# Holding back SyncE's first loads until earlier ones have landed, in a conditional MLP kernel

## What is computed

```
out_nr = gelu(x @ w1_nr + b1_nr) @ w2_nr + b2_nr
out_tsr = gelu(x @ w1_tsr + b1_tsr) @ w2_tsr + b2_tsr
h = gelu(gelu(x @ w1_sr + b1_sr) @ w2_sr + b2_sr)
out_sr = h @ w3_sr + b3_sr
y = x + (out_nr, out_tsr or out_sr, by the batch's condition)
out = (y - mean(y)) * rsqrt(var(y) + 1e-5) * gamma + beta
```

## Time and profile before

| | us |
|---|---|
| median of 3 runs (lowest, highest) | 559.55 (559.47, 559.73) |
| the profiled execution, its own time | 559.85 |
| its span, first to last instruction | 558.1 |
| TensorE busy | 549.3 (98%) |
| VectorE, GpSimd, ScalarE busy | 273.9, 249.7, 213.4 |

### The profile page before, as it was taken

How to read it: one execution, slowest core, us unless ns; L and a number is a source line. 1 busy time by engine, 2 the same in 40 slices (tenths; PEclk the granted TensorE clock), 3 DMA queues, 4 the chain that set the end, 5 groups by cost and what they waited for, 6 DMA issues and landing times. The chain is left out here.

```text
span 558.1 us, 8218 instructions
## 1 busy us (share of the span) xinstructions
PE 549.3 (98%) x2423; PEld 452.1 (81%) x2424; DVE 273.9 (49%) x447; ACT 213.4 (38%) x328; POOL 249.7 (45%) x195
## 2 busy tenths in 40 slices
PE   9999999999999999999999999999999999999994
PEld 6878888888888888888888888888888888888883
DVE  5761176875855956114710569112765105501656
ACT  5451336145244354214421452424245124513351
POOL 0979899774674675300430046600174300530056
PEclk9999999999999999999999999999999999999998
DMA  8875405345344443200320044400244101410042
GB/s 313 335 243 188 152 2 189 112 151 177 118 156 165 136 150 141 85 0 0 137 89 0 2 159 140 150 0 0 75 151 161 64 0 32 158 36 0 0 136 91
DMA packets 26226, 61.28 MB, mean 110 GB/s; under 512 B 3042, under 2 KB 3042, under 8 KB 26082
## 3 DMA queue, kind: packets, MB, share of 16 engines
q1 hardware_dynamic: 26208, 61.10, 32.0%
q10 hardware_dynamic: 2, 0.00, 0.0%
HBM read 44.31 MB, written 16.78 MB: 109 GB/s over the span
## 5 line engine op out<-in xcount | busy, mean ns | idle before, releaser
L456 DVE TENSOR_TENSOR g_lo<-bank,g_hi 128x512 fp32r<-128x512 f32 x112 | 77.5, 692 | 249.2 <-DVEq L117 249.2
L406 ACT ACTIVATE g_hi<-bank,bcol 128x512 fp32r<-128x512 f32 x112 | 77.8, 695 | 163.8 <-ACTq L117 162.5
L599 POOL TENSOR_TENSOR rstd<-var_eps,power 128x2 f32<-128x2 f32 x30 | 20.9, 698 | 237.2 <-POOLq L117 237.2
L595 POOL TENSOR_TENSOR y<-y,row 128x512 f32<-128x512 f32 x64 | 97.1, 1538 | 50.3 <-POOLq L117 49.9
L428 ACT ACTIVATE y<-y,rstd 128x512 f32<-128x512 f32 x63 | 42.2, 717 | 166.9 <-ACTq L117 166.9
L238 PE MATMUL bank<-w_hi,g_lo 128*128 128x512 f32 x256 | 99.6, 389 | 0.0
L237 PE MATMUL bank<-w_lo,g_hi 128*128 128x512 f32 x256 | 99.6, 389 | 0.0
L236 PE MATMUL bank<-w_hi,g_hi 128*128 128x512 f32 x256 | 99.6, 389 | 0.0
L236 PE MATMUL bank<-x_hi,w_hi 128*128 128x512 f32 x240 | 93.5, 390 | 0.0
L237 PE MATMUL bank<-x_lo,w_hi 128*128 128x512 f32 x240 | 93.4, 389 | 0.0
L238 PE MATMUL bank<-x_hi,w_lo 128*128 128x512 f32 x240 | 93.4, 389 | 0.0
(11 more groups left out here) (41 smaller groups left out, 577.3 us busy)
## 6 DMA issues: line engine op xcount, KB each, us to landing
y<-x SPq DMA_DIRECT2D x64, 256.0 KB, 3.7
out<-y SPq DMA_DIRECT2D x64, 256.0 KB, 2.5
stage<-x_t SPq DMA_DIRECT2D x31, 512.0 KB, 3.4
w_raw<-weights SPq DMA_DIRECT2D x17, 512.0 KB, 4.5
row<-rows SPq DMA_DIRECT2D x1, 1280.0 KB, 11.7
stage<-x_t SPq DMA_DIRECT2D x2, 256.0 KB, 3.8
w_raw<-weights SPq DMA_DIRECT2D x2, 256.0 KB, 4.3
cond_sb<-cond ACTq DMA_DIRECT2D x1, 0.1 KB
```

The lines of the kernel that those rows point to most:

```text
L406: eng.activation(g_hi[:, slot, :], psum, ACT.Gelu, bias=b)
L456: eng.tensor_tensor(g_lo[:, slot, :], psum, g_hi32[:, slot, :], ALU.subtract).then_inc(s_gs, 1)
L595: eng.tensor_tensor(y[:, t, :], y[:, t, :], row[:, kind, :], ALU.add).then_inc(s_xb, 1)
L599: eng.tensor_tensor(rstd[:, t:t + n], var_eps[:, t:t + n], power[:, t:t + n], ALU.pow).then_inc(s_rstd, n)
```

## The change

Only SyncE's program changes, and in it only waits are added. No load is added, removed or reordered, and no other engine's program differs (except for line numbers).

```diff
                 eng.dma_start(w_raw[:, c, :], weights[0][:, n]).then_inc(s_w_piece[c], 16)
+
+            eng.wait_ge(s_x_piece[0], 16)
             load_x(x_halves[1], 1)
+            eng.wait_ge(s_w_piece[0], 16)
             load_pair(("nr", 1))
+            eng.wait_ge(s_x_piece[1], 16)
             eng.dma_start(bcol[:, :], bias_cols).then_inc(s_const, 16)
-            for item in [("nr", 2), ("nr", 3)] + POOL_FIRST:
-                load_pair(item)
+            load_pair(("nr", 2))
+            eng.wait_ge(s_w_piece[1], 16)
+            load_pair(("nr", 3))
+            for n in range(2):
+                eng.wait_ge(s_loaded["nr", n + 1], 16)
+                load_pair(POOL_FIRST[n])
+            eng.wait_ge(s_loaded["nr", 3], 16)
             eng.dma_start(row[:, :, :].rearrange("p r h -> p (r h)"), rows.rearrange("r h -> (r h)").partition_broadcast(P)
                           ).then_inc(s_rows, 16)
```

## The result

The changed kernel takes 562.64 us median of 6 runs (561.31 to 564.01) against 559.64 of 6 runs of the kernel before (559.45 to 560.21). The ratio is 1.0049, with a 95% interval of 1.0039 to 1.0059: slower by 3.0 us at the medians. The forecast was 559.5 with a range up to 560.3; the case that came nearest was the rival of the short queue, with 561.0 and a chance of 0.10.

What follows compares the result with a forecast made beforehand. TensorE bounds the kernel, so only late loads reaching its gap at 38.72 cost. All loads hidden gives 0.0, sr1 0 alone up to 0.5; taking 0.0 to 0.1 gave 559.5 to 559.6, written 559.5, range 558.7 to 560.3.

Steps and rivals of the forecast that it cites:

- the rival of the short queue: First loads: a short queue makes transfers slow, 5.3 us each; sr1 0 lands 1.4 us later; 561.0 us, chance 0.10.
- What bounds the kernel, and the place of the gap at 38.72: TensorE, busy 549.3 of 558.1 us; its 0.40 us gap at batch 1's second layer takes late loads at full price.
- The head of that chain: Before the gap at 38.72: sr1 0's landing starts GpSimd's unbroken work, so each us later adds a us.
- Early issues: Second half of x, nr 1, nr 2, nr 3 issued later: all hidden, nr 2 at most 0.05 us late.
- the 4.4 us: Upper of two times from issue to landing, 3.3 and 4.4 us, used as the ends of each load's landing.
- sr1 0: First pair for GpSimd, issued at about 10.1, landing 13.4 to 14.5: between hidden and 0.5 us late.
- `row`: Load behind sr1 1, issued at 12.73, landing 17.9 to 19.0, needed by GpSimd at 22.14: hidden.
- The halves and the `y` tiles: Batch 1's loads behind `row`: landings follow the unchanged queue order, at most 0.7 us late with `row`, covered by VectorE's idleness.
- The cover of 0.80 us before 26.90: VectorE's idle 0.80 us before 26.90 was to cover a lateness of 0.7 us of `row` and the loads behind it.
- Relief: First loads: with fewer loads behind them, x and weight pieces land sooner; 0.8 us won, 558.7 us, chance 0.10.
- Too short a queue: The same as the rival of the short queue: 561.0 us, chance 0.10, its sign GpSimd's start after 15.1.
- The two rules of the Trainium skill: DMA queue: ring order means later loads take no bandwidth from earlier ones; issuing early hides fixed cost, by which +0.5 us.

Runs made afterwards that it cites:

- e3_row: Kernel before plus one wait alone, of `row` on pair nr 3; 560.83 us, ratio 1.0018.
- e1: Kernel before plus only the change's four waits on the first x and weight pieces; 560.88 us against 559.80, ratio 1.0018.
- e5: Kernel before, with SyncE also waiting for `row` to land before it issues batch 1's halves and the `y` tiles; 563.72 us, ratio 1.0078.
- e6: Kernel before plus one wait alone, of `row` on pair nr 2; 559.77 us against 559.86, ratio 0.9999.
- e8: Changed kernel with every wait one step back, a window of about six loads; 559.88 us against 559.86, ratio 1.0001.
- e10: Kernel before with sr1 0 and sr1 1 loaded as two halves each, and `row` waiting on pair nr 3; 560.46 us, ratio 1.0004.
- e4: Changed kernel, with SyncE also issuing nothing between `row` and its landing; 566.60 us, ratio 1.0108.
- e7: Kernel before plus one wait alone, of `row` on pair nr 1; 559.77 us against 559.86, ratio 0.9999.
- e9: The changed kernel once more, for a second trace; 563.38 us of 4 runs, ratio 1.0065.

## Why the prediction was wrong, point by point

- **What bounds the kernel, and the place of the gap at 38.72.** Right: the loss shows there and nowhere after. In nine of the traces the distance from VectorE's second residual addition (26.90 before, 29.68 after) to TensorE's second layer is 11.82 to 11.88 us (38.72 - 26.90 = 11.82, 41.51 - 29.68 = 11.83).
- **The head of that chain.** Wrong in part. I took sr1 0 and GpSimd's unbroken work alone for it. VectorE's first residual addition at 25.41 had no idle time in front (the row before it is the low part of the x of batch 1), so the chain also runs through batch 1's halves of x: landing, ScalarE's copy, VectorE's low part from 20.94 to 25.49, then the residual. Here is the row of the kernel before that shows it:

```profile
20.94 4.55 DVE L461 TENSOR_TENSOR x_lo<-stage,x_hi 128x1024 fp32r<-128x1024 f32 x2 [1.67 <-DVEq L117]
25.41 0.68 DVE L471 TENSOR_TENSOR bank<-bank,y 128x512 f32<-128x512 f32 x1
```

 In the changed kernel both heads, the half of x and the additions on the first `y` tile, are 3.5 to 3.9 us late. About 1.1 us of this is got back, since the low part takes 3.46 us instead of 4.55 when GpSimd adds beside it for less of its time (from 25.68 instead of 22.14); 2.79 are left.
- **Early issues** (second half of x, nr 1, nr 2, nr 3). The time from issue to landing was over the 4.4 us in all of them: 5.5, 5.3, 5.5 and 6.2 us. For the first two the order of the queue hid nearly all of it: the half of x was used at 9.01 instead of 8.79, nr 1 at 10.33 instead of 10.08. Nr 2 was not hidden. It was used at 12.48, 1.0 us late, and nr 3, behind it, at 13.72 instead of 12.73.
- **sr1 0.** It was issued at 10.32 and landed 4.6 us later, just outside the 4.4; its term of at most 0.5 us measured 1.0.
- **`row`: the term that was mis-sized most.** I gave it a start-up of 3.3 to 4.4 us beside the transfers ahead of it and full rate after, landing at 17.9 to 19.0 when issued at 12.7. From its true issue at 13.7 that would be 18.9 to 20.0. It landed at 22.3: 2.3 us beyond the upper end for itself, and 1.0 for the issue that came late because nr 3 landed late. The step that failed is "As long as the next load is ready before the one ahead of it is through, its late issue costs nothing". e3_row is its test: with `row` issued 2.5 us before sr1 1 had landed, the rate from 15 to 18 us was 274 GB/s instead of 404 and the kernel lost 1.0 us. Two things were wrong in the rule. The 16 DMA engines are not through with a load together, so some stood idle from 13.5 us on, and the packets of a `row` issued late took longer, 0.55 instead of 0.39 us.
- **The halves and the `y` tiles.** "The landings follow the order of the queue" was right, and that is why the lateness of `row` went on to all of them, 3.9 us for the first half. I had them late by 0.7 us at most, and priced that at nothing.
- **The cover of 0.80 us before 26.90.** It is no cover. The changed kernel has the same 0.80 us at 29.68, with everything before it 2.8 us later, and so have e1, e3, e5, e6, e8 and e10. The traces show what VectorE waits for: in all fourteen its second residual addition starts 0.26 us after the end of GpSimd's second addition on `y`. And that addition is itself held up by VectorE. In the eleven traces in which VectorE's low part of x reaches into it, it takes 2.26 to 2.27 us and ends 1.14 to 1.15 us after that low part; in the three in which the low part is over before it starts (e4, e7, e9) it takes 1.28 to 1.29 us, and the idle time is 0.56. Here it is in the kernel before and in e7_row_nr1:

```profile
24.37 2.27 POOL L595 TENSOR_TENSOR y<-y,row 128x512 f32<-128x512 f32 x1
```

```profile
25.89 1.28 POOL L598 TENSOR_TENSOR y<-y,row 128x512 f32<-128x512 f32 x1
```

 So the idle time moves along with VectorE's own work in front of it.
- **Relief.** It did not happen: the second pieces are used at 6.63 and 7.36 against 6.67 and 7.49, and the first weight piece later, at 4.98 against 4.56.
- **Too short a queue.** This came nearest to the mechanism, and its sign (GpSimd's start after 15.1) was there, at 15.13. But its path was sr1 0 alone. I had its evidence, 233 GB/s with two pairs in flight and 256 at the start, and set it aside with a count: nine loads issued and not landed at 6 us as at 14 us, one slow and one fast. Both counts are right; they say that the number of loads in flight does not set the rate. What also differed was how long the loads under way had been queued: the second half of x, issued at 2.63, landed at 8.8, and sr1 0, issued before 6.0, at 14.0. That this is why the start is slow was not tried. The price of 561.0 was too low because it counted only sr1 0, which landed at 15.0 and not at 15.4, and not `row` and what follows.
- **The two rules of the Trainium skill.** By the Trainium skill, page "DMA: Bandwidth & Descriptors", section "Queues, rings and completion order", each DMA engine takes the descriptors of a ring in their order. I had concluded that a later load takes nothing from an earlier one on its queue, and agreeing with that, the second pieces were used at most 0.13 us sooner with fewer loads behind them. By section "Rules for kernel authors" of the same page of the Trainium skill, a DMA is to be issued early. It pointed the right way, and I gave it only the fixed cost as its price. The runs show more than that: for the full rate of `row` 5.2 us early is enough, and 3.8 is not.

## What to carry to other kernels

Where a queue of loads is the pacemaker, holding a load back is free only with a margin: here one `wait_ge` on SyncE cost 1.0 us when it let `row` out 2.5 us ahead of its turn, and nothing at 3.8 and 5.2 us ahead, though the rate was back at 404 GB/s only with the last. "Issued before the load ahead has landed" is not the condition to plan for. And before an idle time is counted as cover, ask what its releaser was waiting for: if that leads back to the same engine, the idle time moves along and covers nothing.

## What the runs showed of the hardware

- A 1280 KB load on SyncE's queue takes 3.1 us behind the load ahead of it if it was issued 5 us or more before that one landed (seven traces), and 3.8 to 5.4 us if less than 4 us (seven traces). In e3_row, from 13 to 18 us, about a third of the loss of rate is in idle DMA engines and two thirds are in slower transfers: 277 GB/s at 0.89 busy against 419 at 1.01. For loads of 512 KB no such rule shows.
- The 16 DMA engines don't pass from one load to the next together: the first packet of `row` starts at 13.3 us and the load ahead of it lands at 15.3 (the kernel before).
- Silence on the issuing engine does not help (e4_quiet: 7.9 us to landing, 257 GB/s).
- GpSimd's two-input addition of 128x512 takes 1.28 us, and 2.27 when VectorE makes the low part of x (two inputs in SBUF) beside it (e7_row_nr1 and the kernel before).
- After a gap of TensorE of 2.83 us the granted clock was at the lower level for some 3.4 us (e4_quiet, 0.51 from 46.0 to 49.5 us); after the gaps of up to 1.79 us in the other traces it stayed at the higher one.
- Kernels with a short queue vary more between runs: 561.31 to 564.01 us for the changed kernel, 559.45 to 560.21 for the kernel before beside it.
